# Half of an expert layer's down product as three fp32r products of high and low parts

## The reference, cut to what matters

```python
logits = x_flat @ gate_w.T                      # 1024 x 8
top_v, top_i = jax.lax.top_k(logits, 2)
probs = softmax(top_v)                          # weight of each of the two experts
hidden = silu(x_flat @ wg[e].T) * (x_flat @ wu[e].T)   # 256 -> 1024, for expert e
acc = acc + we[:, None] * (hidden @ wd[e].T)           # 1024 -> 256: the down product
```

## Time and profile before

| what | value |
|---|---|
| median of 3 runs | 629.07 us (628.97 to 629.11) |
| the profiled execution's own time | 628.11 us |
| its span, first to last instruction | 626.2 us |
| PE, weight loads, DVE, ACT, POOL busy | 96%, 82%, 73%, 54%, 43% of the span |
| mean granted TensorE clock | 0.995 of full |

### The profile page before, as it was taken

The page is one execution under the profiler, slowest core; times in us unless marked ns, Lnnn a source line. Parts: engine busy times, 40 slices in busy tenths (PEclk is TensorE's granted clock), DMA queues, the critical chain, the costliest instruction groups (busy, mean ns, idle before and its releaser), DMA issues.

```text
span 626.2 us, 10851 instructions
## 1 busy us (share of the span) xinstructions
PE 602.0 (96%) x4045; PEld 515.7 (82%) x4045; DVE 459.1 (73%) x812; ACT 336.4 (54%) x603; POOL 266.3 (43%) x318
## 2 busy tenths in 40 slices
PE   8999999899999999998999988999999999999995
PEld 6889988898889988996667666888888888888884
DVE  4876678866977698768888967876867667676851
ACT  4547523673257423562867672665564746566550
POOL 4317920684147631695454533124242433324222
PEclk9999999999999999999999999999999999999999
DMA  8978987899969836982000494899999999999742
GB/s 280 341 303 228 272 317 198 228 279 293 306 175 294 238 82 190 225 210 68 2 2 2 156 392 168 320 327 344 334 328 355 328 348 337 354 330 339 240 151 84
DMA packets 66148, 152.89 MB, mean 244 GB/s; under 512 B 7649, under 2 KB 47969, under 8 KB 55201
## 3 DMA queue, kind: packets, MB, share of 16 engines
q1 hardware_dynamic: 61728, 146.04, 70.0%
q0 software_dynamic: 4368, 6.16, 4.9%
HBM read 121.91 MB, written 31.59 MB: 245 GB/s over the span
## 4 chain that ended last, share of the span: by engine, by line
PE 73%; DVE 10%; POOL 7%; DMA 3%; ACT 3%; issue 2%; SPq 0%; POOLq 0%; DVEq 0%; ACTq 0%
PE psum L1700 19%; PE psum L1310 13%; PE psum L1435 13%; PE psum L1717 12%; PE psum L1475 9%; POOL wide_low L605 4%; PE psum L1385 2%; DVE head_max L974 2%; DVE region_a L979 1%; POOL wide_high L603 1%; DMA region_a<-ctx_dram 1%; DMA region_w<-sums_by_token,tokens 1%; PE psum L1518 1%; POOL region_s L625 1%; PE psum L1351 1%
## 5 line engine op out<-in xcount | busy, mean ns | idle before, releaser
L692 ACT ACTIVATE wide_high<-region_a 128x1024 fp32r<-128x1024 f32 (+1 forms) x108 | 107.8, 998 | 97.7 <-PE psum L1700 97.7
L1140 DVE TENSOR_TENSOR wide_low<-region_a,wide_high 128x1024 fp32r<-128x1024 f32 x92 | 112.2, 1221 | 57.9 <-ACT wide_high L692 57.9
L605 POOL TENSOR_TENSOR wide_low<-region_a,wide_high 128x512 fp32r<-128x512 f32 x64 | 82.3, 1289 | 18.3 <-ACT wide_high L692 14.5
L1717 PE MATMUL psum<-region_a,region_w 128*128 128x256 f32 x368 | 83.3, 379 | 0.0
L1475 PE MATMUL psum<-turned_high,wide_low 128*128 128x256 f32 x256 | 79.6, 311 | 2.4 <-DVE turned_low L1051 1.5
L1700 PE MATMUL psum<-wide_low,turned_high 128*128 128x512 f32 x184 | 78.2, 425 | 0.3 <-DVE turned_high L1242 0.2
L1717 PEld LDWEIGHTS psum<-region_a,region_w 128*128 128x128 f32 x368 | 69.7, 190 | 10.2
L1475 PE MATMUL psum<-turned_high,wide_high 128*128 128x256 f32 x256 | 72.4, 283 | 0.0
L1700 PE MATMUL psum<-wide_high,turned_low 128*128 128x512 f32 x184 | 72.3, 393 | 0.0
L1475 PE MATMUL psum<-turned_low,wide_high 128*128 128x256 f32 x256 | 72.2, 282 | 0.0
L1051 DVE TENSOR_TENSOR turned_low<-psum,turned_high 128x512 fp32r<-128x512 f32 x64 | 44.0, 687 | 38.0 <-ACT turned_high L692 38.0
(11 more groups left out here) (221 smaller groups left out, 1226.2 us busy)
## 6 DMA issues: line engine op xcount, KB each, us to landing
region_a<-turned_up SPq DMA_DIRECT2D x23, 2048.0 KB, 9.9
region_a<-turned_down SPq DMA_DIRECT2D x23, 1024.0 KB, 7.1
region_a<-ctx_dram SPq DMA_DIRECT2D x16, 1024.0 KB, 9.2
turned_up<-region_w SPq DMA_DIRECT2D x64, 256.0 KB, 4.0
region_w<-L_ffn_wg_dram SPq DMA_DIRECT2D x16, 512.0 KB, 6.3
region_w<-L_ffn_wu_dram SPq DMA_DIRECT2D x16, 512.0 KB, 6.0
region_w<-L_ffn_wd_dram SPq DMA_DIRECT2D x16, 512.0 KB, 6.0
turned_down<-region_w SPq DMA_DIRECT2D x32, 256.0 KB, 3.9
```

Source lines behind the costliest of these rows:

```text
L605: nc.gpsimd.tensor_tensor(val_lo[:, g % 4], ctx_sb[n][:, g * PAIR:(g + 1) * PAIR, :], val_hi[:, g % 4].bitcast(F32), ALU.subtract).then_in ...
L692: return nc.scalar.activation(dst, src, ACT.Copy)
L1140: nc.vector.tensor_tensor(w_lo[:, k % RING], group_of(k), w_hi[:, k % RING].bitcast(F32), ALU.subtract).then_inc(low_ready, 1)
L1717: last = nc.tensor.matmul(to[:, 0:D], hidT[n][:, ic * P:(ic + 1) * P], rows, start=ic == 0, stop=ic == IC - 1)
```

## The change

In the tiles 0 to 21 (`j < WIDE` = 22) the last four of the eight down products are no longer float32. Their operands are split in a high part in fp32r and a low part, and each float32 product becomes three fp32r products. Tile 22 stays in float32.

- ACT: `tile_step(j)` begins with a copy of the second half of the down weights of tile j - 1 (128x1024) to `down_high_part`, for j from 1 to 22. It waits for the down product of tile j - 2, which last read that buffer, and for the load of the weights. The second copy of `tile_hidT` now goes to `hidT_hi`, in fp32r.
- DVE: `low_down(j - 1)` (128x1024, a subtraction) stands ahead of the low part of group 4j + 3, and `low_hidT(j - 1)` (128x512, a subtraction from PSUM) between the split of the next rows and `tile_hid`.
- PE: the turns of the next tile's hidden columns and the second half of the down product have additional waits for these parts.
- Memory: the two new tensors take the place of `xnT`, which is no longer used once the tokens are routed. `hidT_hi` and `hidT_lo` take the free half of `turned_high` and `turned_low`.

```diff
+WIDE = SLOT_TILES - 1
...
-        xnT = sb("xnT", DC * TOK)[:, :].rearrange("p (c n) -> p c n", c=DC)
+        with nc.sbuf_tensor("xnT", [P, DC * TOK], F32) as until_routed:
+            xnT = until_routed[:, :].rearrange("p (c n) -> p c n", c=DC)
+        HALF = MAT // 2
+        down_hi, down_lo = [sb(name, HALF, F32R)[:, :] for name in ("down_high_part", "down_low_part")]
...
+        hidT_hi, hidT_lo = [t[:, 2 * DC * P:] for t in turned_parts]
...
+        def second_half(j):
+            return w_down[j % 2].rearrange("p (a k h x) -> p h a k x", a=QUADS, k=KPI, h=2)[:, 1]
+
+        def halved(parts):
+            return parts.rearrange("p (a k x) -> p a k x", a=QUADS, k=KPI)
...
             def tile_step(j):
                 n = j % 2
-
+                if 0 < j <= WIDE:
+                    if j == 1:
+                        act.wait_ge(rows_stored, 16 * DUOS)
+                    else:
+                        act.wait_ge(y_done, j - 1)
+                    act.wait_ge(down_loaded[1 - n], 16 * ((j - 1) // 2 + 1))
+                    copy(halved(down_hi), second_half(j - 1)).then_inc(down_high, 1)
                 high(4 * j + 3)
...
             def tile_hidT(j, n):
                 for half in range(2):
                     act.wait_ge(hid_turned, j * 2 + half + 1)
-                    copy(hidT[n][:, half * BANK:(half + 1) * BANK], bank[4 + half]).then_inc(hidT_ready, 1)
+                    to = hidT[n][:, half * BANK:(half + 1) * BANK]
+                    if half == 1 and j < WIDE:
+                        if j > 0:
+                            act.wait_ge(y_done, j)
+                        to = hidT_hi
+                    copy(to, bank[4 + half]).then_inc(hidT_ready, 1)
...
+            def low_down(j):
+                dve.wait_ge(down_high, j + 1)
+                nc.vector.tensor_tensor(halved(down_lo), second_half(j), halved(down_hi.bitcast(F32)), ALU.subtract).then_inc(down_low, 1)
+
+            def low_hidT(j):
+                dve.wait_ge(hidT_ready, j * 2 + 2)
+                nc.vector.tensor_tensor(hidT_lo, bank[5], hidT_hi.bitcast(F32), ALU.subtract).then_inc(hidT_low, 1)
+
             for j in range(SLOT_TILES):
                 n = j % 2
+                if 0 < j <= WIDE:
+                    low_down(j - 1)
                 low(4 * j + 3)
...
+                if 0 < j <= WIDE:
+                    low_hidT(j - 1)
                 tile_hid(j, n, 0)
...
                 if j > 0:
                     pe.wait_ge(hidT_ready, j * 2)
+                    pe.wait_ge(hidT_low, j)
...
-                    last = nc.tensor.matmul(to[:, 0:D], hidT[n][:, ic * P:(ic + 1) * P], rows,
-                                            start=ic == 0, stop=ic == IC - 1)
+                    cols = slice(ic * P, (ic + 1) * P)
+                    if ic < TPG or j >= WIDE:
+                        last = nc.tensor.matmul(to[:, 0:D], hidT[n][:, cols], rows, start=ic == 0, stop=ic == IC - 1)
+                    else:
+                        if ic == TPG:
+                            pe.wait_ge(down_low, j + 1)
+                            pe.wait_ge(hidT_low, j + 1)
+                        cols = slice((ic - TPG) * P, (ic - TPG + 1) * P)
+                        for m, (held, w) in enumerate(((hidT_hi, down_lo), (hidT_hi, down_hi), (hidT_lo, down_hi))):
+                            rows = w.rearrange("p (a k q c r) -> p q k c a r", a=QUADS, k=KPI, q=QUADS // 2, c=DC)[:, (ic - TPG) // KPI, ic % KPI]
+                            last = nc.tensor.matmul(to[:, 0:D], held[:, cols], rows, start=False, stop=ic == IC - 1 and m == 2)
```

More of the change, by code:

```diff
@@ L274, in perceiver @@
         p3_done, p3_act = sem("p3_done"), sem("p3_act")
+        down_high, down_low, hidT_low = sem("down_high"), sem("down_low"), sem("hidT_low")
         behind_ready, gate_exp = sem("behind_ready"), sem("gate_exp_done")
```

## The result

The changed kernel takes 631.51 us (median of 5 runs, 630.66 to 632.17) beside 629.07 for the kernel before: ratio 1.004, 95% interval 1.0022 to 1.0057. It is slower by 2.4 us, where 623.7 was forecast. The profiled execution took 632.17 us, its span is 630.4. It is the slowest of the five, and the profiled one of before (628.11) was faster than that kernel's median, so the two profiles lie 4.1 us apart and the medians 2.4.

A forecast was written before the change was run, and what follows sets the result against it. PE was taken to set the pace, about 10.05 us a tile. Twenty down products gaining 0.285 us give 5.70, less 0.32 at tile 20: 629.07 - 5.38 = 623.7 us, range 622.0 to 626.6.

The forecast's parts named there:

- PE's products: Second half of the down product: twelve fp32r products take 1.44 us instead of 1.725, gaining 0.285 us a tile.
- rival 2: PE's twelve new products: runs of 32 values stream at float32 speed, losing 0.865 us a tile; 647 us, chance within 0.11.
- The rule on weight loads: Loads overlap running matmuls only where the row group differs; twelve products would take 2.57 us; rejected for the attention row.
- The copy of the down weights: ACT, head of each step: 1.06 us, hidden in idle time, price nothing; the weights' load lands 1.9 us early enough.
- It is hidden, with 0.2 to spare: DVE's 1.14 us subtraction for the down weights: over at 506.3, before 506.50, where DVE ended a 1.98 us wait.
- The scaled result, which in the middle nobody waits for urgently: DVE's scaling of each tile's down product: moved 0.59 us later by the hidden columns' subtraction, at no cost mid-stage.
- The end: Tile 20: DVE free at 604.87, so its own gain is lost and 0.32 us more; three DMAs behind unchanged.
- Rival 1 (DMA): Weight loads: DMA engines become the bound, backlog eats the slack, last 7 or so tiles gain nothing; 625.7 us, chance 0.14.
- the others: Also: DVE becomes the bound (628.9) or change does nothing (629), together 0.07; products at 0.108 us each (620.8), 0.05.
- The slower outcome: Kernel slower than before, chance 0.11: products at float32 streaming speed, or at paces between 0.144 and 0.216 us each.
- the sum: Whole kernel: 5.70 us gained in 20 down products, less 0.32 at tile 20, net 5.38; forecast 623.7 us, chance 0.63.

## Why the prediction was wrong

- **PE's products: right.** 1.44 us for twelve, 1.73 for the float32 four, a period of 9.76. Runs of 32 values are streamed at full pace, so rival 2 is out. The rule on weight loads in the Trainium skill ("TensorE: Matmul & The Clock Gate", Part 3, "The mechanism"), weighed in the prediction, is out here too: twelve take 1.44 us, not the 2.57 estimated from the page.
- **ACT: right.** The copy of the down weights waits for PE, never for a load.
- **DVE: right for DVE, and there lay the first mistake.** "It is hidden, with 0.2 to spare": the subtraction does fit into DVE's gap. But I asked only who waits for DVE, not who works during that gap. POOL does, from 504.60 to 508.58, and a DVE subtraction with both operands in SBUF holds it up. The trace before hinted at it: the free gather issues took 0.95 us, those that began while a low part ran 1.75. The Trainium skill names it ("SBUF — State Buffer", "Who interferes with whom": a DVE instruction with two SBUF inputs contends with a GpSimd instruction that reads SBUF). The pause, which reads SBUF, agrees: 1.09 and 1.19 against 0.19 us. I didn't bring that rule to the prediction; it would have made POOL's chain a rival.
- **"The scaled result, which in the middle nobody waits for urgently": wrong, and this is the step that failed.** Behind it stand the pause, the scatter and, in the same queue, the gather of a later tile's rows, with 1.8 us of slack in the example above. A result 0.6 later, a pause up to 1.0 and an issue up to 1.1 longer, and a landing 1.8 later in the median use that up. The prediction put this path at nothing; it cost 8.2 us of waits in eight tiles, and 1.0 in the pause of the end. Of POOL's queue I had costed no step.
- **The end: half right.** In the tile before, where DVE waits for PE, the scaling begins 0.20 us after PE's next product (597.76 against 597.56); for tile 20 it is 0.83 (608.15 against 607.32), so DVE is 0.63 late, where 0.60 was worked out (604.87 against 604.27). The blocked pause, 1.0, was missing.
- **Rival 1 (DMA) wrong, the others too**: weight loads stayed off the chain. The slower outcome had a chance of 0.11 and was tied to the wrong mechanism. Where the hold-up or the late gather is taken away, in four different ways, the kernel takes 623.5 to 624.0, ratios 0.990 to 0.993, beside the 623.7 and 0.991 of the sum: the terms that I had were right to a microsecond or so, and one was missing.

## What to carry to other kernels

When work is put into an idle gap of one engine, list who else works in that gap and what the two share, not only who waits for the result. For each indirect DMA, read its slack from issue, landing and first use, and follow the queue in front of it: an urgent load behind a patient store inherits all the store's waits, and should go first where buffers allow. A new kernel that misses a well-founded sum by several microseconds may be one exchange of two instructions away from it.

## What the runs showed that was not expected

A POOL indirect DMA's issue is lengthened, too, by DVE subtractions with two SBUF operands: 2.38 to 2.69 us in all 21 tiles with float32 products, against 1.59, and back to 1.59 with one operand from PSUM. But it isn't enough that they overlap. Set two low parts of DVE in the changed kernel beside the scatter of 508.43 and the gather of 502.44 above:

```profile
502.57 1.22 DVE L1163 TENSOR_TENSOR wide_low<-region_a,wide_high 128x1024 fp32r<-128x1024 f32 x1
...
507.90 1.23 DVE L1163 TENSOR_TENSOR wide_low<-region_a,wide_high 128x1024 fp32r<-128x1024 f32 x1
```

The scatter began while the second one ran and took 2.16 us, until 1.46 us after its end. The gather had begun 0.13 us before the first one, ran beside it for 0.86, and took 0.99 as if alone. All twelve traces say the same, from 400 to 612 us. Of POOL's instructions that began while DVE ran a 128x1024 subtraction with both operands in SBUF, 78 of 78 pauses ended 0.05 to 0.15 us after it, 138 of 138 gather issues 0.85 to 0.94 and 63 of 64 scatter issues 1.4 to 1.5. The others took 0.18 to 0.20, 0.98 to 1.00 and 1.55 to 1.65, though such a subtraction began during 7, 52 and 179 of them. So in these runs POOL was held where it came second and not where it came first. DVE's subtractions took 1.21 to 1.27 us either way. That is why, from tile 1 on, the pause alone was held in the kernel before with a subtraction and the issue alone with float32 products. In the changed kernel and with early gathers alone the landings stay at 8.6 us once POOL runs late, even in tiles in which the issue takes 1.59 (early gathers: median 1.586), while with an issue held up in every tile but at the old period they are at 6.1. So the landing depends on more than the issue's record: on what DVE does after it, or on where in the tile it falls. Which of these it is wasn't tried, so the step from a late POOL to a late landing stays open; that the subtraction causes the loss, and that the late gather carries it, is shown.
